# Last mixture: the first two gathers of the middle rows land in another buffer, and the bias products move behind the first four contractions

## What is computed

```
x = x + _L1_ffn_ref(_layernorm(x), P_w, U1, U2, U3, W1, W2, b2)

x_addr = x @ P_w.T                       # routing scores
dw1, dw2, dw3 = route(x_addr @ U1.T), route(x_addr @ U2.T), route(x_addr @ U3.T)   # 3 of 12, softmax
h = sum_e dw1[:, e] * (x @ W1[e].T)      # 256 -> 1024
h = gelu(h)
y = sum_e dw2[:, e] * (h @ W2[e].T)      # 1024 -> 256
y = y + dw3 @ b2
```

## Time and profile before

| | |
|---|---|
| median of 3 runs | 1160.59 us (1159.93 to 1161.48) |
| span of the profiled execution | 1216.9 us |
| what lies around the span | no view shows it |
| profiled span over the median | 56.3 us |
| first product, half 1 (756 to 839 us) | 83 us |
| middle rows and second product, "first" turns (839 to 989 us) | 150 us |
| "second" and "whole" turns (989 to 1190 us) | 201 us |
| load back and add (1190 to 1217 us) | 27 us |

### The profile page before, as it was taken

The page is one execution under the profiler, slowest core; times in us unless marked ns, Lnnn a source line. Parts: engine busy times, 40 slices in busy tenths (PEclk is TensorE's granted clock), DMA queues, the critical chain, the costliest instruction groups (busy, mean ns, idle before and its releaser), DMA issues.

```text
span 1216.9 us, 19171 instructions
## 1 busy us (share of the span) xinstructions
PE 1094.3 (90%) x6013; PEld 817.2 (67%) x6013; DVE 552.3 (45%) x1120; ACT 420.3 (35%) x833; POOL 381.8 (31%) x421
## 2 busy tenths in 40 slices
PE   7999899998999999999399999998677888888885
PEld 4888744888998878887244443444566777776773
DVE  4988766764444446776872501333122211111114
ACT  1566544321112225664244432332222232222220
POOL 0221100000220011011154434552666646665650
PEclk8999999998999999999599999998898899999998
DMA  7000130004980029001155578997778865444437
GB/s 208 2 0 0 33 139 1 1 1 161 345 286 9 0 66 382 27 0 47 37 180 200 186 211 295 349 364 276 249 253 278 269 201 179 134 131 142 132 121 281
DMA packets 93410, 187.89 MB, mean 154 GB/s; under 512 B 14109, under 2 KB 34575, under 8 KB 93340
## 3 DMA queue, kind: packets, MB, share of 16 engines
q1 hardware_dynamic: 65346, 109.45, 25.4%
q0 software_dynamic: 23696, 73.69, 19.6%
q10 hardware_dynamic: 4298, 3.81, 1.0%
HBM read 133.56 MB, written 55.44 MB: 155 GB/s over the span
## 4 chain that ended last, share of the span: by engine, by line
PE 40%; issue 4%; DMA 4%; DVE 2%; another core or an unknown queue 2%; ACT 1%; SPq 0%; POOL 0%; POOLq 0%; DVEq 0%; ACTq 0%
PE f_psY L2089 18%; PE f_psH L2046 15%; PE f_psV L2072 4%; DMA W<-in_f_W1T 2%; DMA W<-p_d 2%; PE f_psT L2034 1%; ACT a_W L2146 1%; DVE W L1650 1%; PE f_psV L83 1%; DMA shared<-h_d,f_half_toks 0%; PE f_psH L1929 0%; PE f_psV L1662 0%; SPq L2343 0%; DVE f_xTk L2268 0%
## 5 line engine op out<-in xcount | busy, mean ns | idle before, releaser
L2089 PE MATMUL f_psY<-W,a_W 128*128 x944 | 240.7, 401 | 57.4 <-issue 35.6
L2089 PEld LDWEIGHTS f_psY<-W,a_W 128*128 128x128 f32 x944 | 179.4, 200 | 87.0 <-issue 65.4
L2046 PE MATMUL f_psH<-W,f_xTk 128*128 x472 | 215.5, 596 | 5.7 <-ACT shared L2141 2.0
L2046 PEld LDWEIGHTS f_psH<-W,f_xTk 128*128 128x128 f32 x472 | 84.1, 190 | 96.0 <-issue 95.6
L2146 ACT ACTIVATE a_W<-f_psV 128x512 f32<-128x512 f32 x118 | 70.0, 598 | 155.8 <-PE f_psV L2072 94.8
L2141 ACT ACTIVATE shared<-f_psH 128x512 f32<-128x512 f32 x118 | 70.4, 597 | 142.1 <-PE f_psH L2046 109.5
L1692 POOL DMA_INDIRECT W<-p_d,f_rows x96 | 95.0, 989 | 64.7 <-issue 24.7
L1692 POOL DMA_INDIRECT shared<-h_d,f_half_toks x90 | 87.6, 974 | 85.4 <-DMA p_d<-shared 25.6
L2246 DVE TENSOR_SCALAR a_W<-W,f_wt 128x512 f32<-128x512 f32 x32 | 15.9, 496 | 204.7 <-DMA W<-p_d,f_rows 147.6
L2268 DVE TENSOR_TENSOR f_xTk<-f_psY,f_xTk 128x256 f32<-128x256 f32 x52 | 21.7, 424 | 144.1 <-PE f_psY L2089 112.5
L1692 POOL DMA_INDIRECT a_W<-xn_d,f_toks x59 | 57.6, 975 | 88.9 <-PE f_psT L2034 54.3
(11 more groups left out here) (299 smaller groups left out, 1867.8 us busy)
## 6 DMA issues: line engine op xcount, KB each, us to landing
p_d<-shared SPq DMA_DIRECT2D x118, 256.0 KB
W<-in_f_W1T SPq DMA_DIRECT2D x24, 512.0 KB, 8.8
W<-in_f_W2T SPq DMA_DIRECT2D x24, 512.0 KB
m_wg<-in_m_Wg SPq DMA_DIRECT2D x16, 512.0 KB, 4.0
m_wu<-in_m_Wu SPq DMA_DIRECT2D x16, 512.0 KB, 5.2
m_wd<-in_m_Wd SPq DMA_DIRECT2D x16, 512.0 KB, 6.1
h_d<-a_W SPq DMA_DIRECT2D x32, 256.0 KB
W<-p_d SPq DMA_DIRECT2D x16, 384.0 KB, 9.2
```

What stands on the lines that cost most here:

```text
L2046: mm = pe.matmul(psH[:, n % 2, :], xTk[:, i, k, :], W1[c][:, e, k, :], start=k == 0, stop=k == KD - 1)
L2089: mm = pe.matmul(psY[:, n % 2, 0:D], hT[:, m % 2, k, :], W2[c][:, e, k, :], start=k == 0 and not (whole and c == 1), stop=k == KQ - 1 and ...
```

## The change

It has three parts. The "first" turns take seat (i + 5) % 7, so h(0) and h(1) land in `sel`, and GpSimd issues these two ahead of the wait for all product stores. The bias products are made in groups of four, behind C(0) to C(3). Their four PSUM banks are now `psT` and `psH` (the expansions' banks) instead of `psT` and `psY`, which the contractions now use meanwhile. The wait for the bias products in front of seat 4 thereby moves from h(4) to h(6).

```diff
+BIASES = 4
...
-                            seats = (i % (DEEP if kind == "first" else QUAD + 1),)
+                            seats = ((i + QUAD + 1) % DEEP if kind == "first" else i % (QUAD + 1),)
...
-                    bias_banks = [psT[:, 0, 0:D], psT[:, 1, 0:D], psY[:, 0, 0:D], psY[:, 1, 0:D]]
+                    bias_banks = [psT[:, 0, 0:D], psT[:, 1, 0:D], psH[:, 0, 0:D], psH[:, 1, 0:D]]
...
                                 wait(pool, hT_mm, u.free)
-                                if u.kind == "first" and u.tile == QUAD:
+                                if u.kind == "first" and u.seat == QUAD and u.use == 1:
                                     pool.wait_ge(b_mm, TT)
...
+                            all_sums(0)
+                            for n in range(DEEP - QUAD - 1):
+                                hidden(n)
                             all_products(1)
-                            all_sums(0)
-                            for n in range(QUAD):
+                            for n in range(DEEP - QUAD - 1, QUAD):
                                 hidden(n)
...
                                 pe.wait_ge(dwT_ready, 1)
+                                pe.wait_ge(po_ready, 2 * LT)
                                 pe.wait_ge(b2_ld, 16 * (P // EP))
...
                                 if n < 2:
-                                    pe.wait_ge(b_done, TT)
+                                    pe.wait_ge(dwT_ready, 1)
...
-                            for i in range(TT):
-                                bias(i)
                             turn_hidden(0)
                             for m in range(TILES):
                                 if m + 1 < TILES:
                                     turn_hidden(m + 1)
                                 contract(m)
+                                for i in range(BIASES * m, min(BIASES * (m + 1), TT)):
+                                    bias(i)
```

## The result

| | changed kernel | kernel before, same chip |
|---|---|---|
| median of 6 runs | 1168.11 us (1165.64 to 1173.72) | 1161.60 us (1159.93 to 1162.60) |
| ratio | 1.0065 [1.0046, 1.0083] | |
| profiled execution | 1165.64 us, span 1163.8 us | |

The change makes the kernel slower by 0.65%, 7.5 us by the ratio (the two medians lie 6.5 us apart). The sign was forecast; the size was forecast at half of it (+3.8 us), and the median lies just above the range.

What follows compares the result with a forecast made beforehand. TensorE was taken to bound the kernel up to 839 us, then mostly GpSimd's gathers and scatters. Between TensorE's pace (-0.8 + 2.5 = +1.7 us) and GpSimd's (+2.3 + 2.5 = +4.8), +3.8 gave 1164.4 us, range 1158.6 to 1168.0.

Steps and rivals of the forecast that it cites:

- The start of the second product: Start of the second product: h(0) issues near 835, T(0) and T(1) run at 839.5 to 840.8, T(2) at 846.9.
- the dip I charged to T(2) and C(1): Half-rate clock of TensorE at about 842 to 849, slowing T(2) and C(1) by 0 to 2.4 us, taken as 1.0.
- T(2) 5.6 us sooner: Start of the second product: T(2) at 846.9 instead of 852.5, with h(2) issued at 843.07 after the product stores.
- The stand at h(6): GpSimd waits 4.8 us (2.1 to 7.5) at h(6) for the bias products; its chain is 2.3 us later.
- The seam: Where 'second' turns begin: h(52) waits for T(51) instead of T(49), so T(52) starts 2.5 us later.
- The sum: Whole kernel: +1.7 us if TensorE sets the pace, +4.8 if GpSimd does; +3.8 taken, giving 1164.4 us.
- two thirds of the way: Whole kernel: the forecast's place between TensorE's pace (+1.7 us) and GpSimd's (+4.8), giving +3.8.
- Heavier: Rival: GpSimd bound, half clock, bias products at VectorE's pace: 4.4 + 2.5, +6.9 us, 1167.5; 0.15 together with no effect.
- TensorE bound: Rival: TensorE sets the pace after 839 us, the stand is made up: +1.7 us, 1162.3; 0.27 together with a cheap seam.
- A cheap seam: Rival at h(52): late sums hold it longer than T(51) does; +2.3 us or less, 1162.9; 0.27 together with TensorE bound.
- Faster: Rival: early start survives, clock full, h(6) issued by 854.5, T(6) 2.9 us sooner, seam under 0.6 us: 1157.8; chance 0.13.
- The change does not do what it says: Rival: last sum of half 0 stored too late, so h(0) gains nothing and the kernel is slower; chance 0.03.

Runs made afterwards that it cites:

- h0_before: The kernel before, unchanged, run again for its profile on a chip of the short kind (1160 us).
- h2_b16_loose: Changed kernel with all 16 bias products behind C(0) and the 'second' seats shifted by one: 1.0002 of the kernel before, short chip.
- g3_after: The changed kernel, unedited, timed again on a short chip: 1.0080 of the kernel before.
- h1_stand: Changed kernel with the 'second' seats shifted by one, bias products still in fours: 1.0034 of the kernel before, short chip.
- g4_front_loose: Changed kernel with bias products in front of T(0) and the 'second' seats shifted by one: 1.0003 of the kernel before, short chip.
- b0: The kernel before, unchanged, run again for a profile on a long chip: 1212.84 us, span 1211.0.
- e2_front: Changed kernel with the bias products in front of T(0), 'second' seats as in the change: 1.0029 of the kernel before, long chip.
- g1_before_tight: Kernel before with 'second' turns on seat (i + 2) % 5, so h(52) waits for T(51): 1.0034 of the kernel before, short chip.

## Why the prediction was right in sign and half in size

**The start of the second product.** h(0) was to issue near 835 and T(0), T(1) to run from 839.5 without a wait. h(0) did issue early, but 1.3 us less early than forecast: it followed the last sum's store by 4.3 us (828.97 to 833.26) instead of 3.0. It landed after 5.0 us instead of 3.8 (833.26 to 838.29), and T(0) waited 1.76 us for it. C(0) then ran mostly at half clock, 3.26 us: the dip I charged to T(2) and C(1) with 1.0 us came earlier, as the stretch 840 to 844 with a clock of 0.63 shows. The Trainium skill's rule that half rate is the default ("TensorE: Matmul & The Clock Gate", Part 1) agrees with this row: the clock fell after TensorE had stood for 1.76 us and for 0.48.

"T(2) 5.6 us sooner" rested on product stores seen at an unchanged time. They weren't: the first gather after them issues 3.45 to 3.54 us after the copy of the last product starts in all five traces of the old order (h0_before 3.50), and 4.44 to 5.04 in all fifteen with the early gathers, whether the bias products lie in front, in groups or all behind C(0) (841.00 - 836.56 = 4.44 in the changed kernel). So with two gathers going early the product stores are seen 0.9 to 1.6 us later; that the gathers' traffic holds them up is a guess that no run tests. T(2) came 8.7 us after the copy, against 12.9 in the profile before (11.7 to 14.1 in the other four traces of the old order): 4.2 us sooner, not 5.6. And the saving that I put at 2.5 us for two gathers is 1.4 on GpSimd's row: h(7) issues 15.8 us after that copy instead of 17.25 where there is no stand (h2_b16_loose, h0_before). The short chips' medians don't show even this (1.0002 and 1.0003); why is open.

**The stand at h(6).** Its mechanism, place and releaser were right: 4.8 us forecast, 5.68, 6.20 and 4.71 measured on short chips (changed kernel, g3_after, h1_stand). These waits hold the usual 0.3 us of issue, so the forecast's 4.8 stands against 5.4, 5.9 and 4.4. The bias group added 0.79 us to each step, with 0.73 forecast; what was off is the smaller saving, above all, and the 0.8 us from the last bias product's start (854.36) to h(6). Net on GpSimd's row it is 3.5 to 4.8 us (h(7), against h0_before), not +2.3.

**The seam.** Right in mechanism (h(52) released by T(51), T(52) waiting for it), mis-sized at 2.5 us, with 3.0 to 3.2 in its better form and 6.0 to 6.6 in the other. The parts: release to issue 1.38 us instead of 0.87; 3.1 to 5.1 us from issue to use over the eight traces instead of 3.8; the 0.6 us by which T(53) falls back behind T(52), put at nothing; and the half clock after a long wait, which I hadn't considered here. That T(52) itself is 2.5 us late in the short form, as forecast, is luck: 1.38 + 3.3 happens to equal 0.87 + 3.8. The 1.38 could have been read before. The 0.87 was taken from h(54), while h(52) in the same trace was released by T(49), at

```profile
999.32 0.60 PE L2072 MATMUL f_psV<-ident,shared 128*128 128x128 f32 x4
```

and issued at 1000.70, 1.38 us later. The Trainium skill's formula ("DMA: Bandwidth & Descriptors", Anatomy of one DMA), by which T(52) would wait 1.3 us, is further off; none of the eight landed in its 2.6 us.

**The sum.** The step that failed is the size of the two waits. The stand, less the two gathers saved, was put at +2.3 us and cost +3.9; the seam was put at +2.5 and cost +4.3. Together that is +8.2 us, against the 7.5 that the ratio gives. A smaller error lies on top: "two thirds of the way" between TensorE's and GpSimd's pace took 1.0 us off, where on the chip of the timing both waits count in full. At GpSimd's full pace the forecast would have been +4.8, still 2.7 short. My own rule, 56 us of waits that an ordinary execution lacks, pointed to GpSimd, and even then I held on to a profile whose engines wait for things no row shows.

Three figures of the working don't follow from its terms. The earliest end of the bias products comes to 853.7, not 853.9. With 4.2 and 2.4 us in place of 2.2 and 1.0 the stand's upper bound is 8.2 us, not 7.5. And the 4.4 us of "Heavier" would be 5.7.

The rival "Heavier" (+6.9) came closest, and for another reason than it gave: not the bias at VectorE's pace but a longer way from issue to use.

**The rivals.** "TensorE bound" fell with h1_stand and h2_b16_loose, on the short chips. "A cheap seam" fell: the seam costs the same in front of either start. "Faster" would have needed both waits gone; with both gone (g4_front_loose, h2_b16_loose) the time equals that of before, 1.0003 and 1.0002. "The change does not do what it says" fell with h(0) at 833.26.

The best version of the idea, the early gathers with a loose seam and the bias products in one place, is 0.27% faster on one long chip, not clearly so on the other, and the same on the short ones. It doesn't beat the kernel before where that takes 1160 us.

## What to carry to other kernels

When a change rotates a table of buffers, recount for every later user how many steps lie between the one that frees the seat and the one that fills it; here one constant turned two steps into none, at the one place where the order changes kind, and it cost as much as the stand. Starting one engine sooner is worth only what the engine that paces the stage gains: ask first which engine's issues follow one another without a gap, and put any new wait elsewhere. And if the profiled execution is 5% longer than the median, its slack is not the slack of the runs that are timed.

## What was not expected of the hardware

- Chips differ by 5% on the same program: the kernel before took 1159.4, 1159.6 and 1161.6 us on three, and 1216.4, 1217.2 and 1222.4 on three others. On the long ones ScalarE and TensorE have waits that nothing in the trace ends, of up to 12.1 us (b0) and 10.9 us (e2_front); why was not tested. Each chip was met in one set only, so chip and moment are not told apart.
- With two gathers issued ahead of pending stores, those stores are seen about 1.3 us later, in each of the fifteen traces that have them.
- The same gather, h(52) behind T(51), is used 3.1 to 3.3 us after its issue in five traces and 4.8 to 5.1 in three.
- After an idle time of 3.8 to 4.1 us in front of T(52), C(51) took 3.4 to 3.8 us instead of 1.89 (g1_before_tight at a granted clock of 0.50, g3_after, e2_front); after one of 2.1 to 2.4 us, in the other five traces, it took 1.99. The length of the idle time alone doesn't decide: C(0) of the changed kernel took 3.26 us after waits of 1.76 and 0.48.
